# Context products with the keys stationary, probabilities normalised on GpSimd before their transpose, low parts of the queries on VectorE

## What is computed

```
q_big  = rope(einsum('bshk,hkq->bshq', x_norm @ Wq.T, w_kc_q))     # 192 per head
kv_r   = rope(kv_c)                                                # 64
scores = (q_big @ W_qr) . (kv_r @ W_kr)                            # 256 x 256 per batch and head
attn   = softmax(scores, axis=-1)
ctx_c  = attn @ kv_r                                               # 64 per head
out    = (ctx_c @ w_kc_kv.T, heads joined) @ Wo.T
```

## Time and profile before

| | us |
|---|---|
| median of 3 runs | 550.41 (549.96 to 551.56) |
| the profiled execution | 551.55 |
| its span in the trace | 549.70 |
| rounds 1 to 7 of the loop | 268 of it |
| round 8 | 31.0 |
| PE busy | 434.3 (79%) |
| DVE busy | 337.7 (61%) |
| ACT busy | 206.2 (38%) |
| POOL busy | 184.7 (34%) |
| mean granted clock of PE | 0.86 |

### The profile page before, as it was taken

One profiled execution on the slowest core, in us unless ns is written; L12 is line 12 of the kernel. 1 busy time (PEld: TensorE's weight loads), 2 busy tenths in 40 slices (PEclk: granted clock), 3 DMA queues, 4 the chain that ended last, 5 costly groups with the idle time before them and its releaser, 6 DMA issues.

```text
span 549.7 us, 6341 instructions
## 1 busy us (share of the span) xinstructions
PE 434.3 (79%) x2214; PEld 339.8 (62%) x2215; DVE 337.7 (61%) x714; ACT 206.2 (38%) x412; POOL 184.7 (34%) x117
## 2 busy tenths in 40 slices
PE   2776898898898889888988899993805425979997
PEld 2555787786787778777877788852303214434375
DVE  5566648556767758569475643356839876575232
ACT  1312543553565465346445453023056122321100
POOL 1543423423434253245244511943038520130000
PEclk9868888897898899889988999995965556898999
DMA  8423020020020020000300003100000000000001
GB/s 335 157 87 144 1 77 1 0 77 1 1 79 0 1 78 0 2 0 1 102 4 1 2 0 86 52 0 1 1 0 0 0 1 0 2 0 1 0 30 48
DMA packets 8943, 18.86 MB, mean 34 GB/s; under 512 B 2128, under 2 KB 6672, under 8 KB 7760
## 3 DMA queue, kind: packets, MB, share of 16 engines
q1 hardware_dynamic: 8912, 18.46, 9.6%
HBM read 17.40 MB, written 1.05 MB: 34 GB/s over the span
## 4 chain that ended last, share of the span: by engine, by line
PE 58%; DVE 27%; issue 8%; ACT 3%; POOL 2%; DMA 1%; SPq 0%; POOLq 0%; DVEq 0%; ACTq 0%
PE bank L1151 7%; PE bank L1051 6%; PE bank L1053 5%; PE bank L1052 5%; PE bank L1166 5%; PE bank L1329 5%; PE bank L1127 4%; PE bank L1347 4%; PE bank L1138 4%; DVE rot_z L711 3%; DVE uT L758 2%; PE bank L1080 2%; PE bank L1162 2%; DVE rot_z L709 2%; PE bank L1074 2%
## 5 line engine op out<-in xcount | busy, mean ns | idle before, releaser
L518 ACT ACTIVATE prob<-bank,negmax 128x256 f32<-128x256 f32 x128 | 53.6, 470 | 97.6 <-DVE negmax L750 97.6
L750 DVE TENSOR_REDUCE negmax<-bank 128x2 f32<-128x512 f32 x64 | 43.8, 686 | 52.1 <-PE bank L1127 52.0
L1151 PEld LDWEIGHTS bank<-kva,probT 128*128 128x128 f32 x512 | 67.5, 197 | 4.2 <-issue 0.7
L1151 PE MATMUL bank<-kva,probT 128*128 128x65 f32 x512 | 66.5, 274 | 0.3 <-ACT probT L511 0.3
L394 POOL TENSOR_TENSOR qr<-rot_z,qr 128x512 fp32r<-128x512 f32 x14 | 18.0, 1289 | 102.0 <-ACT qr L534 102.0
L511 ACT COPY probT<-bank 128x512 f32<-128x512 f32 x64 | 37.9, 593 | 38.3 <-PE bank L1138 37.9
L1127 PE MATMUL bank<-kvT,uT 128*128 128x256 f32 x256 | 51.0, 326 | 0.1
L385 POOL TENSOR_TENSOR rot_low<-rot_low,rot_up 128x1024 f32<-128x1024 f32 x16 | 38.0, 2374 | 34.0 <-DVE rot_up L705 34.0
L1051 PE MATMUL bank<-xnT,w 128*128 128x512 f32 x96 | 44.3, 462 | 5.0 <-DVE kvT L772 4.7
L388 POOL TENSOR_TENSOR qr<-rot_low,qr 128x1024 fp32r<-128x1024 f32 x14 | 32.9, 2351 | 39.3 <-ACT qr L527 39.3
L1329 PE MATMUL bank<-tailT,blobs 128*128 128x512 f32 (+1 forms) x96 | 45.3, 629 | 0.8 <-ACT tailT L477 0.8
(11 more groups left out here) (189 smaller groups left out, 884.1 us busy)
## 6 DMA issues: line engine op xcount, KB each, us to landing
blobs<-in_blob SPq DMA_DIRECT2D x8, 1024.0 KB, 6.5
xs<-in_x SPq DMA_DIRECT2D x2, 512.0 KB, 4.1
ctxT<-in_ctx_t SPq DMA_DIRECT2D x1, 1024.0 KB, 13.6
xn<-in_w_fc_t SPq DMA_DIRECT2D x1, 1024.0 KB, 5.0
ctxT<-in_w_proj_t SPq DMA_DIRECT2D x1, 1024.0 KB, 6.5
out<-qk SPq DMA_DIRECT2D x8, 128.0 KB, 1.7
cb<-in_const_b SPq DMA_DIRECT2D x1, 768.0 KB, 9.5
blobs<-in_w_gate SPq DMA_DIRECT2D x1, 704.0 KB, 4.5
```

The lines of the kernel that those rows point to most:

```text
L518: ins = act.activation(prob[n % 2][:, st, :], pS[n % 2][:, st * S:(st + 1) * S], ACT.Exp, bias=negmax[:, n % 2, st:st + 1])
L750: dve.tensor_reduce(negmax[:, n % 2, :], pS[n % 2][:].rearrange("p (a s) -> p a s", a=2), AX, ALU.max, negate=True).then_inc(max_ready, 1)
L1151: ins = pe.matmul(pV[:, (2 * st + h) * (DC + 1):(2 * st + h + 1) * (DC + 1)], probT[n % 2][:, lt, st * P:(st + 1) * P], kva[:, 2 * b + lt, :],
```

## The change

1. **Context.** Each unit has two products instead of four: a 128-column window of `kva` is stationary, and 256 columns of `probT` move. `kva` is laid out as blocks of 64 columns, rows of context between zeros, so that the window puts head 0 in rows 0 to 63 of the result and head 1 in rows 64 to 127; the four products of a batch add up in one bank (`pV[b % 2]`). The result is already turned, and DVE copies it to `cT` once the second head is in. `turn_context`, the scaling of the context and `cn_all` are gone.
2. **Sums and normalising.** The sum of the exponentials is an accumulated output of ACT's exponential. DVE inverts it (128 x 2), and POOL multiplies `prob` in place (128 x 512, second operand broadcast) before PE turns it. `prob` has three buffers instead of two.
3. **Slots.** `turn_probs(k)` moves from slot k+2 to k+3, `context(k)` and ACT's copy of `probT` from k+3 to k+4. ACT's cast of `rot_z` is a slot earlier.
4. **Low parts.** For all groups DVE subtracts the high parts; POOL keeps the joins alone.
5. **Set-up.** `kva` is cleared whole, and `ones` and `pad` lie in table space that is read out by then.

The diff, cut:

```diff
-            def join(n):
-                pool.wait_ge(rot_ready, RT * n + 2)
-                pool.tensor_tensor(rot_low[:], rot_low[:], rot_up[:], ALU.add).then_inc(joined, 1)
-                if n >= 2:
-                    pool.wait_ge(rope_high, 2 * n + 1)
-                    pool.tensor_tensor(qr[n % 2][1][:, 0:2, :], rot_low[:], qr[n % 2][0][:, 0:2, :].bitcast(F32),
-                                       ALU.subtract).then_inc(rope_low, 1)
...
+            def norm_probs(n):
+                pool.wait_ge(sum_turned, n + 1)
+                p = prob[n % PROBS]
+                pool.tensor_tensor(p[:], p[:], rinv[:, n % PROBS, :].unsqueeze(2).to_broadcast([P, 2, S]),
+                                   ALU.mult).then_inc(normed, 1)
...
+            for it in range(1, PAIRS + 1):
+                for slot in range(SLOTS):
+                    m = QSTEPS * it + slot // 2
+                    if 2 <= slot <= NUNIT + 1:
+                        norm_probs(NUNIT * (it - 1) + slot - 2)
+                    if slot % 2 == 1 and m < ALLQ and m % RT:
+                        join(m // RT, m % RT - 1)
...
-                    if g >= 0 and 3 <= slot <= NUNIT + 2:
-                        n = NUNIT * g + slot - 3
+                    if g >= 0 and 4 <= slot <= NUNIT + 3:
+                        n = NUNIT * g + slot - 4
                         act.wait_ge(probsT_ready, n + 1)
...
-                            ins = act.activation(prob[n % 2][:, st, :], pS[n % 2][:, st * S:(st + 1) * S], ACT.Exp,
-                                                 bias=negmax[:, n % 2, st:st + 1])
+                            ins = act.activation(prob[n % PROBS][:, st, :], pS[n % 2][:, st * S:(st + 1) * S], ACT.Exp,
+                                                 bias=negmax[:, n % 2, st:st + 1],
+                                                 accum_out=rsum[:, n % PROBS, st:st + 1])
...
+                    if g >= 0 and 2 <= slot <= NUNIT + 1:
+                        n = NUNIT * g + slot - 2
+                        dve.wait_ge(probs_ready, n + 1)
+                        dve.reciprocal(rinv[:, n % PROBS, :], rsum[:, n % PROBS, :]).then_inc(sum_turned, 1)
...
+                    if slot % 2 == 1 and m < ALLQ and m % RT == 2:
+                        rope_lows(m // RT, 0)
+                    if slot % 2 == 1 and RT <= m < ALLQ + RT and m % RT == 0:
+                        rope_lows(m // RT - 1, 1)
...
-                        in_order(dve.reciprocal(rsum[:], pv[:, :, DC]))
-                        if n >= 2:
-                            dve.wait_ge(cT_ready, n - 1)
-                        dve.tensor_tensor(cn[n % 2].rearrange("p a (h d) -> p (a h) d", h=2), pv[:, :, 0:DC],
-                                          rsum[:].unsqueeze(2).to_broadcast([P, 4, DC]), ALU.mult).then_inc(cn_ready, 1)
...
-                        dve.wait_ge(cT_ready, B * g + b + 1)
-                        dve.tensor_copy(cT[:, g, b * S:(b + 1) * S], pC[:, 0:S]).then_inc(cT_copied, 1)
+                        dve.wait_ge(pv_ready, NUNIT * g + 2 * b + 2)
+                        dve.tensor_copy(cT[:, g, b * S:(b + 1) * S], pV[b % 2][:, 0:S]).then_inc(cT_copied, 1)
...
-                if h == 0 and n:
-                    pe.wait_ge(cn_ready, B * g + b)
-                for st in range(2):
-                    for lt in range(2):
-                        ins = pe.matmul(pV[:, (2 * st + h) * (DC + 1):(2 * st + h + 1) * (DC + 1)],
-                                        probT[n % 2][:, lt, st * P:(st + 1) * P], kva[:, 2 * b + lt, :],
-                                        start=(lt == 0), stop=(lt == 1))
+                if h == 0 and B * g + b >= 2:
+                    pe.wait_ge(cT_copied, B * g + b - 1)
+                for lt in range(2):
+                    ins = pe.matmul(pV[b % 2][:, 0:S], kva[:, (2 * (2 * b + lt) + 1 - h) * DC:(2 * (2 * b + lt) + 1 - h) * DC + P],
+                                    probT[n % 2][:, lt, :], start=(h == 0 and lt == 0), stop=(h == 1 and lt == 1))
                 ins.then_inc(pv_ready, 1)
...
-            def turn_context(g, b):
-                n = B * g + b
-                pe.wait_ge(cn_ready, n + 1)
```

More of the change, by code:

```diff
@@ L43 @@
 PREPS = 4
+PROBS = 3
 QSTEPS = 2 * RT
@@ L411, in _ @@
             in_order(ins)
-            pool.tensor_tensor(kva[:, :, 0:DC], kva[:, :, 0:DC], kt.rearrange("p b a d -> p (b a) d"),
-                               ALU.add).then_inc(kva_ready, 1)
-            for n in range(1, GROUPS):
-                join(n)
+            in_order(pool.tensor_tensor(kv_rows, kv_rows, kt.rearrange("p b a d -> p (b a) d"), ALU.add))
+            pool.memset(ones, 1.0)
+            pool.memset(pad, 0.0).then_inc(kva_ready, 1)
+            join(1, 0)
+            join(1, 1)
+            for it in range(1, PAIRS + 1):
[5 more added lines that the diff above has]
+                        join(m // RT, m % RT - 1)
             pool.wait_ge(d_mask, 32)
@@ L527, in _ @@
                         act.copy(qr[n % 2][0][:, 0:2, :], rot_low[:]).then_inc(rope_high, 1)
-                    if slot % 2 == 1 and RT <= m < ALLQ + RT and m % RT == 0:
+                    if slot % 2 == 0 and RT <= m < ALLQ + RT and m % RT == 0:
                         n = m // RT - 1
@@ L713, in rope, with rope_lows @@
                 ins.then_inc(rot_ready, 1)
-            def first_lows(n, half):
+            def rope_lows(n, half):
                 dve.wait_ge(rope_high, 2 * n + half + 1)
@@ L1193, in _ @@
                             latent_u(n, 2)
-                    if g >= 0 and slot >= 5 and slot % 2 == 1 and (slot - 5) // 2 < B:
-                        turn_context(g, (slot - 5) // 2)
                     if it == PAIRS and 1 <= slot:
@@ L1206, in _ @@
                             project(t, pair)
-                    if g >= 0 and 3 <= slot <= NUNIT + 2:
-                        if it == 1 and slot == 3:
+                    if g >= 0 and 4 <= slot <= NUNIT + 3:
+                        if it == 1 and slot == 4:
                             pe.wait_ge(kva_ready, 1)
-                        context(g, slot - 3)
+                        context(g, slot - 4)
                     if f + 1 < PAIRS and slot in (1, 3, 5, 7):
@@ L1216, in _ @@
                         pe.wait_ge(wkvo_ready, it + 2)
[L1217 removed]
+                        pe.transpose(pW[:, 0:P], pad, ident).then_inc(wmax_turned, 1)
                     if it == 2 and slot == 11:
                         pe.wait_ge(wdiag_ready, 1)
[L1220 to L1222 removed]
+                        pe.matmul(pW[:, P:P + 2], ones, wdiag[:], start=True, stop=True).then_inc(wmax_here, 1)
+                    if g >= 0 and 3 <= slot <= NUNIT + 2:
+                        turn_probs(g, slot - 3)
             pe.wait_ge(wkvo_ready, PAIRS)
```

93 lines of the change are left out of this document (34 added, 59 removed).

## The result

The changed kernel takes 520.81 us (median of 4 runs, 520.40 to 522.28) against 550.18 for the kernel before in the same session: a ratio of 0.948, 95% interval 0.944 to 0.952.

What follows compares the result with a forecast made beforehand. PE was taken to lead, a 37.9 us round being 4.0 of waits, 3.4 of low clock and 30.5 of work. Savings by round of 11.6 us from 551.55 gave 539.9, stated as 539 for the median; range 523 to 553.

Steps and rivals of the forecast that it cites:

- The low clock behind slot 5: PE after its gap in slot 5: low clock stays, so a steady round takes 36.9 us instead of 35.2.
- the rival of the full clock: PE's clock stays full behind the gap of slot 5: seven rounds save 1.7 us each, 530 us; chance 0.20.
- The low clock of slot 11 is no gain of its own: Low clock behind slot 11's wait: its removal gains nothing by itself, as DVE sets slots 0 to 5.
- The gate, T + 16.2: Slot 5: context(1) starts 16.2 us after the round's first latent_q product, behind normalising, join, cast, folded weights and copy.
- The gap ahead of it, 3.0: PE ahead of context(1) in slot 5: nothing to do from about T + 13.2, a gap of 3 us.
- Behind the gate, 19.0: From context(1) in slot 5 to the next round: 17.9 us of work plus 1.1 of new waits on PE.
- The context product and the turns: PE: four context records take 0.86 us against 0.84 before; the four turns that go save 0.9 us a round.
- Low parts: DVE gets 3.3 us of low parts a round; one of 128 x 512, 0.6 us, lies ahead of the gate.
- not the bound as a sum: DVE's total work, with low parts, inverses and lost work counted, is 28.5 us of a 36.9 us round.
- The port: DVE and POOL collide on their shared port in slots 11 and 3 and at inverses: 19.8 us, 559; chance 0.11.
- The later gate: POOL's normalising takes 2.4 us instead of 1.3, delaying join, cast, copy and PE: 7.7 us, 547; chance 0.15.
- The rounds: Savings by round: 3.7 us in rounds 1 and 2, 4.0 in 3 to 6, 2.5 in 7, 1.4 in 8.

Runs made afterwards that it cites:

- slot 5 filled: Kernel before with four unused products put on PE ahead of the context's turn of slot 5 alone, rounds 1 to 7: 536.25 us, ratio 0.973.
- the wait put back: Changed kernel with context(7) of slot 11 also waiting for DVE's low part, which stands behind rot_z: 537.57 us, ratio 0.977.
- unit 1 twice: Changed kernel with an extra POOL multiplication by one ahead of the normalising of unit 1, rounds 2 to 8: 529.51 us, ratio 0.963.
- the join first: Changed kernel with POOL's join of rot_low ahead of the normalising of its slot instead of behind it: 523.46 us, ratio 0.953.

## Why the prediction was wrong

The direction and the chain that leads to the gate were right; the length of PE's gap there, and with it the clock, were not.

- **The low clock behind slot 5: this step failed.** "With the low clock behind the gap of slot 5 ... it is 36.9", and the full clock (35.2) had 0.20. A steady round takes 33.9, at a granted clock of 1.00. Of the 3.0 us between, 1.7 is the stretch that did not come, 0.9 the gate and 0.4 the work behind it; so the rival of the full clock, with 35.2 a round, missed too. The stretch rested on a gap of 3.0 us, and the gap was 1.4 (below). And where a gap of 2 us did stand, it brought the stretch less surely than the 13 of 14 of the kernel before: alone in its round 5 of 7 times there, and in the changed kernel 1 of 4 at 2.04 us and 2 of 4 at 2.40. A gap of 3.0 us in this place was not run; those of 3.38 us and more that the traces have in rounds 1 to 8 all had low clock behind them.
- **"The low clock of slot 11 is no gain of its own": wrong.** In the kernel before with slot 5 filled, a stretch there costs 1.5 us (36.26 against 34.76), in the changed kernel with the wait put back 1.0 and 1.5. DVE waits for PE's first products there, and I had the 0.9 for this in the very next step (T + 2.5 becomes T + 1.6), inside a sum that ended at T + 16.2 by other additions. It is no less real for being spent.
- **The gate, T + 16.2: it came at T + 15.3.** DVE's maximum of unit 3 ended at T + 11.6 (I had 12.3), the join ran T + 10.5 to 13.3 (11.5 to 13.9). The normalising took 1.04 undisturbed against 1.3 taken and 1.2 as the lower bound. That is 0.9 us in each of rounds 3 to 6.
- **The gap ahead of it, 3.0: it was 1.4.** The gate accounts for 0.9. The other 0.7 is on PE, which ran out of work at T + 13.9 and not at 13.2: I left a wait out of its list, the 1.1 us for which the preparation product of slot 3 waits for DVE itself. One gap of 3 became two of 1.1 and 1.4. No wait of 1.7 us or less in rounds 1 to 8 had low clock behind it in any of these traces, so the shorter gap fits the full clock; the split alone was not put to a test.
- **Behind the gate, 19.0: 18.6 measured** (202.69 to 221.28). Slot 11's new wait is 0.67, forecast 0.8; its old one is gone, as forecast. Slot 7's 0.3 does not show.
- **The context product and the turns: right.** Four records took 0.86 us.

```profile
206.79 0.86 PE bank L1144 x4
```

  That is 215 ns a record again, and a product is two records. The Trainium skill ("TensorE: Matmul & The Clock Gate", "Back-to-back issue gap") gives 109 ns for 256 columns; by the row it does not hold for a record of this type, as the prediction had taken it.

- **Low parts: mis-sized.** I counted 0.6 of them ahead of the gate, which is what they cost a steady round (33.9 against 33.3 without), but set it against other terms and wrote "not the bound as a sum" for the rest. By itself part 4 is a loss of 6.0 us in the change. No share of busy time shows that: DVE is at 27.7 of 33.9 us.
- **Rivals.** The port did not decide: ahead of the gate the collision is there (a normalising of 1.41 and a join of 2.81 where alone they take 1.04 and 2.37), but what collides is DVE's fp8 piece, as it did before. In slot 11 the low part went first and the join waited, the other way round than this rival needed (POOL's L375 at 186.89 took 2.32 us, DVE's L721 at 186.84 took 1.23).

```profile
196.45 1.41 POOL L382 TENSOR_TENSOR prob<-prob,rinv 128x512 f32<-128x512 f32 x1 [1.70 <-DVE rinv L756]
197.00 1.42 DVE L817 SCALAR_TENSOR_TENSOR wpr<-bf_m,ctxT 128x512 bf16<-128x512 bf16 x1
197.82 2.81 POOL L377 TENSOR_TENSOR rot_low<-rot_low,rot_up 128x1024 f32<-128x1024 f32 x1
198.93 0.15 DVE L756 RECIPROCAL rinv<-rsum 128x2 f32<-128x2 f32 x1
```

  An inverse in the middle of the join took 0.15 us, and DVE's maximum ahead of it 0.68, as always: the inverses do not stand behind POOL. Here the Trainium skill ("SBUF — State Buffer", "Who interferes with whom") is borne out; it does not name the inverse among what takes the shared pair. The later gate was the right mechanism (unit 1 twice moved PE's wait by the full 1.0 us), but it went the other way.
- **The rounds:** 1 and 2 lost 8.4 together (forecast 3.7), 3 to 6 lost 17.2 (4.0), 7 lost 4.4 (2.5), the last round 2.2 (1.4).

## What to carry to other kernels

A wait on PE costs its length and what the clock does behind it, and here the second was the larger part of the gain; fill the wait with products of no use to read that price before moving any work. Before forecasting a clock, write down every gap that is left and compare its length and number with gaps that the trace shows, not with the one that goes. In a change of several parts, price each part at the gate it passes: moving the low parts to the busier engine cost a sixth of what the rest brought (6.0 of 35.4 us), and only its own experiment showed it.

## What the runs showed that I had not expected

- Gaps of PE of about 2 us were followed by low clock, mostly for about 4 us and sometimes for 7 (a granted clock of 0.50 to 0.71 over the next 4 us), but not each time: 13 of 14 with two in a round, 5 of 7 with one at either place; in the changed kernel 1 of 4 at 2.04 us and 2 of 4 at 2.40 in slot 5, 3 of 5 at 2.21 in slot 11. Waits of 1.7 us and less in rounds 1 to 8 brought none. The wait for `rot_low` in round 2 is the plainest case: it is 1.75 to 1.80 us in nine of the kernels, and low clock followed in three (the changed one, unit 1 twice, the join first) and not in six. So one profiled execution can differ from another of almost the same kernel by a stretch, 1.5 us. What decides is open.
- POOL's multiplication of 128 x 512 with the broadcast inverse takes 1.04 us, less than the 1.29 of the subtraction of that shape; in the mean over the kernel it is 1.20, by the port:

```profile
L382 POOL TENSOR_TENSOR prob<-prob,rinv 128x512 f32<-128x512 f32 x64 | 76.9, 1202 | 104.3 <-DVE rinv L756 104.2
```
